# Three cross-attention stages: products of two units in turn over the parts of the array, in half groups, with the masked keys shared between two engines

## The reference

```python
x = x + jnp.tanh(g_xattn[l]) * _Ll_xattn_ref(_layernorm(x), ctx_768, ...)
x = x + jnp.tanh(g_ffn[l])   * _Ll_ffn_ref(_layernorm(x), ...)
```

```python
q, k, v = split_heads(x @ Wq), split_heads(ctx @ Wk), split_heads(ctx @ Wv)
attn = softmax(einsum('bhqd,bhkd->bhqk', q, k) * scale)
out = einsum('bhqk,bhkd->bqhd', attn, v).reshape(...) @ Wo
```

## Time and profile before

| | |
|---|---|
| median of three runs | 1204.11 us |
| the profiled execution | 1200.54 us |
| its span, first to last instruction | 1198.8 us |
| busy in the span: TensorE, weight loads | 847.0 us (71%), 691.8 us |
| VectorE, ScalarE, GpSimdE | 712.7 (59%), 440.8, 271.0 us |
| chain that ended last | PE 57%, DVE 25%, POOL 5% |
| mean granted TensorE clock | 0.834 |

### The profile page before, as it was taken

How to read it: one execution, slowest core, us unless ns; L and a number is a source line. 1 busy time by engine, 2 the same in 40 slices (tenths; PEclk the granted TensorE clock), 3 DMA queues, 4 the chain that set the end, 5 groups by cost and what they waited for, 6 DMA issues and landing times.

```text
span 1198.8 us, 22952 instructions
## 1 busy us (share of the span) xinstructions
PE 847.0 (71%) x8147; PEld 691.8 (58%) x8150; DVE 712.7 (59%) x1737; ACT 440.8 (37%) x961; POOL 271.0 (23%) x310
## 2 busy tenths in 40 slices
PE   1336346057995693999856799928999999729981
PEld 0215132045774682677636699926777777629870
DVE  5866868964565335676675356565566666463334
ACT  1441419113443352355414433313434443206550
POOL 1000000000000572344300577500000000007771
PEclk9659677577996796899957899967999999658995
DMA  7300000006001118100001111180000000001114
GB/s 202 90 1 1 1 0 1 0 1 159 1 1 36 36 54 220 40 1 0 1 0 36 34 48 48 38 233 3 2 1 0 0 0 1 27 12 54 50 52 120
DMA packets 72964, 48.05 MB, mean 40 GB/s; under 512 B 19546, under 2 KB 65636, under 8 KB 72900
## 3 DMA queue, kind: packets, MB, share of 16 engines
q1 hardware_dynamic: 64484, 31.80, 9.9%
q0 software_dynamic: 6464, 13.25, 3.5%
q10 hardware_dynamic: 1952, 2.15, 0.6%
HBM read 33.74 MB, written 13.43 MB: 39 GB/s over the span
## 4 chain that ended last, share of the span: by engine, by line
PE 57%; DVE 25%; POOL 5%; issue 4%; DMA 4%; ACT 4%; ACTq 0%; DVEq 0%; POOLq 0%; SPq 0%; another core or an unknown queue 0%
PE ps L2071 8%; PE ps L2085 5%; PE ps L1595 5%; PE ps L1854 4%; PE ps L1932 3%; PE ps L1607 3%; PE ps L1879 3%; PE ps L1809 3%; POOL rows_y L544 3%; PE ps L1819 3%; PE ps L1892 2%; POOL arena L539 2%; PE ps L1908 2%; PE ps L1838 2%; PE ps L1863 2%
## 5 line engine op out<-in xcount | busy, mean ns | idle before, releaser
L539 POOL DMA_INDIRECT arena<-rows_x,row_in x101 | 99.3, 983 | 242.9 <-DVEq L1211 213.0
L2071 PE MATMUL ps<-arena 128*128 128x128 f32 x1120 | 148.1, 282 | 0.6 <-ACT arena L1533 0.4
L2071 PEld LDWEIGHTS ps<-arena 128*128 128x128 f32 x1120 | 137.6, 197 | 2.1 <-ACT arena L1533 0.6
L2085 PE MATMUL ps<-arena 128*128 x808 | 110.7, 280 | 8.2 <-DVE arena L1174 8.0
L544 POOL DMA_INDIRECT rows_y<-arena,row_out x101 | 105.3, 1043 | 41.1 <-issue 24.1
L2085 PEld LDWEIGHTS ps<-arena 128*128 128x128 f32 x808 | 99.2, 193 | 13.6 <-issue 13.4
L1160 DVE COPY arena<-arena 128x644 f32 (+1 forms) x101 | 61.0, 604 | 71.7 <-DVE arena L1174 30.2
L1595 PE MATMUL ps<-q,onesb 128*128 128x256 bf16 x482 | 69.2, 284 | 48.5 <-DVEq L854 48.5
L1607 PE MATMUL ps<-ident,xh 128*128 128x128 f32 x128 | 37.1, 449 | 85.1 <-DVE xh L600 69.0
L1413 ACT COPY arena<-ps 128x512 f32<-128x512 f32 (+1 forms) x96 | 49.3, 514 | 119.0 <-PE ps L1879 118.9
L880 DVE TENSOR_REDUCE arena<-ps 128x8 f32<-128x512 f32 (+1 forms) x96 | 57.6, 600 | 58.3 <-PE ps L1854 52.7
(11 more groups left out here) (296 smaller groups left out, 1727.9 us busy)
## 6 DMA issues: line engine op xcount, KB each, us to landing
arena<-rows_y SPq DMA_DIRECT2D x20, 256.0 KB, 4.6
arena<-in_L_ffn_w SPq DMA_DIRECT2D x2, 2048.0 KB, 9.2
arena<-in_L_ffn_w SPq DMA_DIRECT2D x16, 256.0 KB, 6.8
rows_x<-xh SPq DMA_DIRECT2D x3, 1024.0 KB, 5.1
rows_x<-zero SPq DMA_DIRECT2D x1, 2560.0 KB, 9.9
arena<-in_L_ffn_gate_proj SPq DMA_DIRECT2D x8, 256.0 KB, 5.0
arena<-in_L_ffn_up_proj SPq DMA_DIRECT2D x8, 256.0 KB, 4.9
arena<-in_L_ffn_down_proj SPq DMA_DIRECT2D x1, 2048.0 KB, 10.0
```

The lines of the kernel that those rows point to most:

```text
L539: g.indirect_dma_start(xq[:, q % XS, :], None, rows_x, bass.IndirectOffsetOnAxis(row_in[:, q:q + 1], 0)).then_inc(sem(f"xq_loaded{q % XS}" ...
L2071: ins = pe.matmul(ps[:, 2 * m + s_ % 2, P * f:P * f + P], wst[:, s_ % 4, lo:lo + P], xqT[:, s_ % 2, :], start=True, stop=True)
L2085: ins = pe.matmul(ps[:, 4 + s_ % 2, 0:P], hT[:, s_ % 2, f, :], w2[:, P * f:P * f + P], start=(f == 0), stop=(f == NF - 1))
```

## The change

The units of a group are taken two by two. `pair_scores(i, u)` issues the products of units u and u + 1 in turn, so that four parts of the array follow each other, and waits until VectorE has read the scores of both units before. In stage 3 `pair_values` does the same with the value products. In stages 1 and 2 `values` is as before, but two calls of it follow each other, as two turns do. The fillers before each turn go; a run of 6 (stage 1) or 9 (stage 2) stands before each two turns. In stage 2 ScalarE makes the first two masked key copies straight from PSUM, with the mask as scale and a masked bias, and VectorE the last two from PSUM; ScalarE's unmasked key copy goes. In stage 3 the projection writes to bank 7 instead of 6, and the orders of VectorE and ScalarE follow the half groups; its first group is no longer prepared ahead.

```diff
         def keys(i):
             if l != 3:
-                if l == 2:
-                    v.wait_ge(sem("k_biased"), i + 1)
-                    for j in range(n_k):
-                        own(v.tensor_scalar(t["k"][:, j, :], t["ot"], headmask[l][:, j:j + 1], None, ALU.mult),
-                            f"k_ready_{l}")
-                    return
                 v.wait_ge(sem(f"q_ready_{l}"), i + 1)
-                for j in range(n_k):
+                for j in range(NSUB[l] - n_k, NSUB[l]):
                     own(v.tensor_scalar(t["k"][:, j, :], ps[:, 6, GT:2 * GT],
                                         bqk[:, 1:2] if l == 2 else 0.0, headmask[l][:, j:j + 1],
                                         ALU.add, ALU.mult), f"k_ready_{l}")
...
+            scores(i, 0)
+            scores(i, 1)
+            if first:
...
             else:
-                weigh(i, 1)
-                scores(i, 2)
-                if not first:
-                    add_group(i - 1)
-                weigh(i, 2)
-                scores(i, 3)
-                if more:
-                    keys(i + 1)
-                weigh(i, 3)
-                outputs(i, 0)
-                if more:
-                    scores(i + 1, 0)
-                    weigh(i + 1, 0)
-                    scores(i + 1, 1)
-                outputs(i, 1)
+                outputs(i - 1, 1)
+            weigh(i, 0)
+            weigh(i, 1)
...
+                add_group(i - 1)
+            scores(i, 2)
+            scores(i, 3)
+            outputs(i, 0)
+            weigh(i, 2)
+            weigh(i, 3)
+            if more:
+                keys(i + 1)
+            if not first:
+                group_statistics(i - 1)
...
+            v.tensor_scalar(masked_bk[:, :], headmask[2][:, 0:2], bqk[:, 1:2], None, ALU.mult
+                            ).then_inc(sem("masked_bk_ready"), 1)
...
             s.wait_ge(sem(f"q_mm_{l}"), i + 1)
             if l == 2:
-                ins = s.activation(t["q"][:, 0, :], ps[:, 6, 0:GT], ACT.Identity, bias=bqk[:, 0:1])
-                ins.then_inc(sem(f"q_ready_{l}"), 1)
-                s.activation(t["ot"], ps[:, 6, GT:2 * GT], ACT.Identity, bias=bqk[:, 1:2]).then_inc(sem("k_biased"), 1)
-                return
+                s.activation(t["q"][:, 0, :], ps[:, 6, 0:GT], ACT.Identity, bias=bqk[:, 0:1])
+                for j in range(2):
+                    ins = s.activation(t["k"][:, j, :], ps[:, 6, GT:2 * GT], ACT.Identity,
+                                       bias=masked_bk[:, j:j + 1], scale=headmask[2][:, j:j + 1])
             else:
                 ins = s.copy(t["q"][:, 0, :], ps[:, 6, 0:GT])
             ins.then_inc(sem(f"q_ready_{l}"), 1)
...
         def group(i, more, first=False):
             if l == 3:
-                values(i)
+                if not first:
+                    probT(i - 1, 2)
+                    probT(i - 1, 3)
+                    outputs(i - 1, 1)
+                expo(i, 0)
+                values(i, (0, 1))
                 expo(i, 1)
+                values(i, (2, 3))
                 probT(i, 0)
+                probT(i, 1)
+                outputs(i, 0)
                 expo(i, 2)
-                probT(i, 1)
                 if more:
-                    queries(i + 1)
+                    queries(i + 1, (0, 1))
                 expo(i, 3)
-                probT(i, 2)
-                outputs(i, 0)
                 if more:
-                    expo(i + 1, 0)
-                probT(i, 3)
-                outputs(i, 1)
+                    queries(i + 1, (2, 3))
                 return
-            for u in range(3):
-                if not first:
-                    probT(i - 1, u + 1)
-                expo(i, u)
-                if u == 0 and (not isinstance(i, int) or i > 1):
-                    output_T(i - 2)
+            if not isinstance(i, int) or i > 1:
+                output_T(i - 2)
+            expo(i, 0)
+            if not first:
+                probT(i - 1, 2)
+                probT(i - 1, 3)
+            expo(i, 1)
             if more:
                 queries(i + 1)
+            expo(i, 2)
             probT(i, 0)
             expo(i, 3)
+            probT(i, 1)
             values(i)
...
+        fill = {1: 6, 2: 9, 3: 0}[l]
...
-        def scores(i, u):
-            pe.wait_ge(sem(f"s_sub_{l}"), UNITS * i + (u + 1))
+        def pair_scores(i, u):
...
             apart()
             if l != 3:
-                r = 32 * u
                 for c in range(2):
                     for hh in range(2):
                         lo = S * (2 * hh + c)
-                        o = ps[64 * hh:64 * hh + 64, u % 2, 0:2 * sub * S]
-                        ins = pe.matmul(o.rearrange("p (h c s) -> p h c s", c=2, s=S)[:, :, c, :], t["q"][r:r + 32, 0, lo:lo + S],
-                                        t["k"][r:r + 32, :, lo:lo + S], start=True, stop=True)
-            else:
-                r = 64 * (u % 2)
-                for c in range(2):
-                    for k in range(4):
-                        ch = 4 * (u // 2) + k
-                        for hh in range(2):
+                        for b in range(2):
+                            r = 32 * (u + b)
+                            o = ps[64 * hh:64 * hh + 64, b, 0:2 * sub * S]
+                            ins = pe.matmul(o.rearrange("p (h c s) -> p h c s", c=2, s=S)[:, :, c, :],
+                                            t["q"][r:r + 32, 0, lo:lo + S], t["k"][r:r + 32, :, lo:lo + S],
+                                            start=True, stop=True)
+                            if c == 1 and hh == 1:
+                                ins.then_inc(sem("s_mm"), 1)
+                return
+            for c in range(2):
+                for k in range(4):
+                    ch = 2 * u + k
+                    for hh in range(2):
+                        for r in (0, 64):
                             lo = S * (2 * hh + c)
-                            ins = pe.matmul(ps[64 * hh:64 * hh + 64, u % 2, S * (2 * k + c):S * (2 * k + c) + S],
+                            ins = pe.matmul(ps[64 * hh:64 * hh + 64, r // 64, S * (2 * k + c):S * (2 * k + c) + S],
                                             t["q"][r:r + 64, ch, lo:lo + S], t["k"][r:r + 64, ch, lo:lo + S],
                                             start=True, stop=True)
-            ins.then_inc(sem("s_mm"), 1)
+                            if c == 1 and k == 3 and hh == 1:
+                                ins.then_inc(sem("s_mm"), 1)
...
         def turn(i, u):
-            if l != 3:
-                dense(2 + u % 2, 3)
...
+        def pair_values(i, u):
+            pe.wait_ge(sem("pT_ready"), UNITS * i + (UB[l] + u + 2))
+            if u == 0:
+                pe.wait_ge(sem(f"v_ready_{l}"), 4 * i + 4)
+            else:
+                pe.wait_ge(sem(f"o_half_{l}"), 4 * i + 2)
+                pe.wait_ge(sem(f"o_other_{l}"), 4 * i + 2)
             apart()
             for hh in range(2):
                 for k in range(sub):
                     for c in range(2):
-                        r = 64 * c
-                        pt = t["pt"][r:r + 64, u % 2, k, 64 * hh:64 * hh + 64]
-                        h = 2 * (4 * (u // 2) + k) + u % 2
-                        q = 64 * (u % 2)
-                        o = ps[q:q + 64, 4 + c, P * k + S * hh:P * k + S * hh + S]
-                        ins = pe.matmul(o, t["v"][r:r + 64, hh, d * h:d * h + d], pt, start=True, stop=True)
-            if u % 2:
-                ins.then_inc(sem(f"av_mm_{l}"), 1)
+                        for q in (0, 64):
+                            r = 64 * c
+                            pt = t["pt"][r:r + 64, q // 64, k, 64 * hh:64 * hh + 64]
+                            h = 2 * (2 * u + k) + q // 64
+                            o = ps[q:q + 64, 4 + c, P * k + S * hh:P * k + S * hh + S]
+                            ins = pe.matmul(o, t["v"][r:r + 64, hh, d * h:d * h + d], pt, start=True, stop=True)
+            ins.then_inc(sem(f"av_mm_{l}"), 1)
...
+        def finish_older(i):
+            older = not isinstance(i, int) or i > 1
+            if older:
+                outputs_T(i - 2)
+            values(i - 1, 0)
+            values(i - 1, 1)
+            if older:
+                project_out(i - 2)
+            dense(3, fill)
+            turn(i - 1, 2)
+            turn(i - 1, 3)
         def group(i, first=False, more=True):
             if l != 3:
-                for u in range(3):
-                    scores(i, u)
...
-                scores(i, 3)
+                pair_scores(i, 0)
+                if first:
+                    dense(3, 36)
+                else:
+                    finish_older(i)
+                pair_scores(i, 2)
                 if more:
                     queries_keys(i + 1)
-                dense(2, 24 if first else 8)
-                turn(i, 0)
                 if not first:
+                    values(i - 1, 2)
```

(34 more changed lines are left out.)

79 lines of the change are left out of this document (32 added, 47 removed).

## The result

The changed kernel takes 1151.67 us (median of four runs, 1147.07 to 1154.00) beside 1203.59 of the kernel before: a ratio of 0.956, 95% interval 0.952 to 0.960. The forecast was 1171, in a range of 1158 to 1190. So the sign was right and the size wrong: 52 us instead of 33, outside the range.

A forecast was written before the change was run, and what follows sets the result against it. TensorE's own list of work with its waits was taken to bound the attention stages. Gains of 7.4, 8.4 and 17.2 us in stages 1 to 3 sum to 33.0, off the 1204.11 median: 1171.1, range 1158 to 1190.

The forecast's parts named there:

- 13 records in flight: Where stage 3's first two units overlap in the earlier trace: 13 of a possible 16, taken as near the lower price end.
- the first rival: All stages: strict program-order starts make each pair cost two units, no gain from turns; net 5.0 us, 1199; chance 0.12.
- ScalarE's V copies: Stages 1 and 2: value products newly wait for ScalarE's copies of V, 1.1 and 1.05 us a group.
- VectorE's key copies: Stage 3: third key product waits for key copies standing behind VectorE's weighing, 1.0 us a group, bounds 0.3 to 1.8.
- The masks: Stage 2 key masks shared by VectorE and ScalarE: cost zero, or 0.5 us a group without idle cover.
- pairs: Two units' products in turn cost 0.62, 1.10, 1.20 us in stages 1, 2, 3, saving 1.08, 1.84, 3.84 a group.
- fillers: Fewer filler products a group: 20 become 12 in stage 1, saving 1.08 us; 18 in stage 2, saving 0.43.
- other waits: Stage 3, each group: value products' wait for output copies minus 0.5 us, V's products' wait for ScalarE plus 0.3.
- second rival: Waits are longer than counted because hand-overs are joint; half of the 33 us is given back, 1187; chance 0.19.
- the better case: Pairs at the lower bound and key copies in time: 10 us more gain, 1161; included in the forecast's 0.60.
- a loss of 1: Stage 3's last group: TensorE has nothing left while VectorE weighs the last two units, about 1 us lost.
- third rivals: Granted clock falls to half in stages 1 and 2, 5.5 us lost per group, 1210 or more; chance 0.09.

## Why the prediction missed

**What held.** TensorE's own list with its waits bounds the stages. Overlap of units is real: the reading of 13 records in flight was right, and the first rival (a pair at two units' price, 1199) is refuted by 1.02 to 1.09 us a pair. This also answers the Trainium skill's rule (TensorE: Matmul & The Clock Gate, Part 3, Packing small matmuls) that matmuls are strictly first in, first out in their starts and ends. The traces differ in the starts: a value record starts at 902.24 ahead of six score records that stand before it. As a price rule it fails too: strict order would make turns of one cost two units, 2.16 (1.05 measured). That order matters from turns of eight on (1.05, 1.05, 1.50, 1.76) is what is left of it. The waits came where they were named: ScalarE's V copies (shown by their removal) and VectorE's key copies (the same). The masks cost nothing.

**The terms of a steady group**, forecast against measured, in us:

| | stage 1 | stage 2 | stage 3 |
|---|---|---|---|
| pairs | -1.08 / -1.13 | -1.84 / -2.00 | -3.84 / -4.50 |
| value products (1, 2), transposes (3) side by side | 0 / -0.19 | 0 / -0.17 | 0 / -0.40 |
| fillers | -1.08 / -1.07 | -0.43 / -0.43 | |
| full-size products behind another kind of product | 0 / +0.19 | 0 / +0.19 | 0 / +0.29 |
| new wait (1, 2: V copies; 3: key copies) | +1.1 / +0.56 | +1.05 / +0.57 | +1.0 / +0.64 |
| other waits | | | -0.2 / -0.42 |
| sum | -1.05 / -1.64 | -1.2 / -1.84 | -3.0 / -4.4 |

Three terms were mis-sized. First, **the pairs**: taken at 1.20 in stage 3, measured 1.02 to 1.09, the lower bound. With all four parts in turn nothing is lost, while I had shaded the bound without a row for the loss. Second, **the wait in stages 1 and 2**, twice too long. I added ScalarE's durations and gaps, 2.5 us from the transposes. In the changed trace TensorE passes the wait 1.95 us after the transposes' start (327.49 to 329.44), though every single duration was right (0.37, 0.42, 0.38). This is ScalarE's timeline there: copy, exponential, copy, the two copies of V.

```profile
327.74 0.37 ACT L1402 COPY arena<-ps 128x256 f32<-128x256 f32 x1 [1.42 <-PE ps L1882]
328.01 0.42 ACT L1398 ACTIVATE arena<-arena 128x256 f32<-128x256 f32 x1
328.33 0.36 ACT L1402 COPY arena<-ps 128x256 f32<-128x256 f32 x1
328.58 0.77 ACT L1433 COPY arena<-ps 64x256 f32<-64x256 f32 x2
```

ScalarE's next instruction starts about 0.1 us before the previous one ends: from start to start a copy takes 0.27 us (327.74 to 328.01) and an exponential 0.32 (328.01 to 328.33). The first copy also starts 0.25 us behind the transposes (327.49), where I had taken 0.4. The trace before has the same spacing, 0.27 from 341.76 to 342.03 and 0.32 from 344.53 to 344.85; I read only the durations. By the Trainium skill (Perfetto Trace Analysis, Summary: the profiler window per engine type) ScalarE's reported window runs through the acknowledgement of the write; the overlaps here agree with that. Third, **runs of equal products**: I took transposes and value products of two units at twice one. Side by side they are cheaper, 0.40 us a group in stage 3 and 0.17 to 0.19 in the others. Against it stands a term that I had at nothing: a projection of stages 1 and 2 took 0.45 us behind transposes and takes 0.64 behind value products. Why isn't tested.

In stages 1 and 2 these terms, times seven, are worth 4.1 and 4.5 us against a difference of 4.6 and 3.2; by parts, the five steady intervals gained 8.2 and 9.0 us, what is ahead of them 2.8 and 2.7, the end 1.0 and -0.1 (there the clock fell at 575.6).

Slips in the working that changed nothing: the two units of the earlier trace rows save 0.32 us (2.23 - 1.91), not 0.2; forecast and second rival add up to 0.79, not 0.80; the 1158 at the low end of the range has no working, the better case gives 1161.

**The larger failure is the count.** Stage 3's terms were multiplied by six intervals, the first group was given nothing and the last a loss of 1. Measured: six intervals 26.0 us (18.2 forecast), first group 6.5 (from the first query product to the second group's V products 40.1, now 33.6), last group 2.5. Both contain pairs like every other, 1.1 us less each. About 3 of the 6.5 are the clock: before, two runs of query products took 5.7 us each instead of 3.8 and a unit 1.97 instead of 1.15, since half clock fell on them (one of the stretches is in the earlier trace rows); in the changed kernel it fell on two pairs, 811.1 to 817.9, and cost 1.6. This part is chance: with stage 3 unchanged, its first interval took 22.1 to 24.1 us in five traces, at clocks of 0.94 to 0.85. That leaves 17.8 us of error for stage 3: 7.8 in the intervals, 10.0 at the ends.

**Given back outside.** Of the 8.1 us, 2.0 can be placed: the router's products behind stage 1. The stretch of these 32 records in the kernel before:

```profile
376.20:381.20 5.00, 4.92 (x32) 4.82 (x32) 0.04 (x1) 1.41 (x2) 0.00 (x0) 0.72 0.65 204
```

And in the changed kernel:

```profile
366.90:373.90 7.00, 6.95 (x32) 6.86 (x32) 0.01 (x1) 1.41 (x2) 0.00 (x0) 0.50 0.45 142
```

They now fall wholly at half clock, where some of them had full clock before. The stretch between stages 1 and 2 is 110.4 us before and 112.0 to 112.8 in all twelve changed traces, so this part stands in every changed trace, against a single trace of before. Of the rest, 2.6 stand ahead of stage 1, where nothing was changed; over the changed traces the whole of it varies by 6 us, and it isn't explained further.

**The second and third rivals.** Longer waits: refuted, they were shorter. The clock: at full level through the steady parts, so this rival didn't come true for this kernel; in stage 2 of others (without fillers, with fillers between the units, unit by unit) it fell.

## What to carry over

In this kernel small products that use parts of the array cost by the busiest part and by how often their sequence is broken: put units on different parts next to each other, and where each has more than a few products, mix them in turns of at most four. Price a chain on another engine from start to start, and count each term over all groups, the first and the last too, with a line of its own for what the clock did there. When a change opens a wait, look where the waited-for engine idles just before: here one moved call gave 11 us in the stages and two moved copies 5, as against 16 for the turns.

## What the runs showed that I had not expected

**The clock falls under full load too.** The kernel with units split by fillers, stage 2, TensorE never idle:

```profile
517.90:521.30 3.40, 3.40 (x29) 2.98 (x26) 1.77 (x5) 0.33 (x1) 1.49 (x1) 0.50 0.03 7
521.30:545.20 23.90, 23.90 (x275) 16.63 (x273) 15.97 (x35) 13.17 (x28) 11.13 (x9) 1.00 0.00 0
545.20:548.60 3.40, 3.40 (x24) 2.98 (x21) 1.62 (x4) 0.16 (x1) 1.49 (x1) 0.50 0.00 0
```

Three times, 27.3 us apart, it goes to half for 3.4 us behind 23.9 us in which TensorE was busy throughout, and three of its intervals take 14.4 instead of 12.8 us. With the pairs unit by unit the clock fell twice in stage 2, also for 3.4 us (intervals of 14.49 and 12.87), behind 11.4 busy of 13.7 us and 19.4 of 20.5. In the changed kernel, with the same work in turns and TensorE idle for 5% of the group, it stayed at 1.00 in the steady groups; so did the version with 12 fillers. Idle time alone doesn't tell when the clock falls; what else does stays open.

**What fillers bought.** In stage 1 nothing: its steady groups kept 1.00 with none and TensorE busy 36.63 of 39.50 us. In stage 2 it isn't settled. In both traces without fillers the clock fell among the steady groups; in the eight with pairs in turn and 12 or 18 fillers a group it stayed at 1.00 there; with fillers between the units, or unit by unit, it fell in spite of them. Two traces are too few to say that the fillers kept it up.
